# Folded K and V products made for two batches at once, evicted by ScalarE and GpSimd

## The chip, the cores and the metric

The kernel runs on one core of a Trainium2 chip. The metric is the device time of one execution in microseconds, lower is better. TensorE is called PE here, VectorE DVE, ScalarE ACT, GpSimd POOL and SyncE SP.

## What is computed

Cross attention and a quantised feed-forward block, each added to its input; x is 8 batches of 1024 tokens of 512 values, the context 8 batches of 64 tokens of 384 values, with 8 heads of 64.

```python
x = x + xattn(layernorm(x), ctx, Wq, Wk, Wv, Wo, bo)
x = x + ffn(layernorm(x), w_gate, w_up, w_down)

# xattn: q = x @ Wq, k = ctx @ Wk, v = ctx @ Wv, per head
#        softmax(q k^T / 8) v, heads joined, @ Wo + bo
# ffn:   bitlinear(silu(bitlinear(x, w_gate)) * bitlinear(x, w_up), w_down)
# bitlinear(x, w): x rounded to integers of -128..127 by its row's maximum,
#                  w rounded to -1, 0, 1 by its mean
```

Because k and v don't depend on x, the kernel folds them. For each batch it makes a 512 x 512 matrix from Wq and k (so that scores = x @ matrix) and one from v and Wo (so that the output = probabilities @ matrix). Each is held as a pair of 16-bit matrices, hi and lo, and so is each operand from x; three products (hi hi, hi lo, lo hi) replace one product in 32 bits.

## The kernel before

The 8192 tokens are 64 tiles of 128 rows, 8 tiles to a batch. After a setup (weights turned into -1, 0, 1, K and V made, first batches folded) a software pipeline runs steps s = -7 to 65. In step s the feed-forward tile is i = s and the attention tile is j = s + 6. Each engine runs one list of pieces in order; `queue` sorts the pieces by a due time, `at(s, f)` for fraction f of step s. A hand-written list, OPENING, comes ahead of everything else and reaches to about the end of step 4: a piece that it doesn't name runs after the whole of it. Engines meet only through semaphores.

A steady step has on PE, in this order: gate_up (tile i, part 0, 8 matmuls of 512 columns), scores (tile j, 12 matmuls), gate_up parts 1 and 2, attend (tile j - 1, 12), gate_up part 3, down (tile i - 1, 16 matmuls): 72 matmuls. DVE: `final` (L949, the last instruction on a tile, which adds the product of `down` to x), two `stats` (L943), `copy_h` (L979), `mult` and `h_part` of part 0 (L957, L961), `x_norm` (L985, normalised x for attention), `s_max` (L992, L996), `mult` part 1, `x_scale` (L1014 to L1022, for the quantised x), `h_part` 1, `e_sum` (L1002 to L1006), `mult` 2, `copy_x` (L1029), `h_part` 2, `add_x` (L1034), `mult` 3, `h_max`. ACT: `quant_h` (L738), `silu` 0 (L729), `x_hi` (L745), `silu` 1, `expo` (L749) between two table loads, `silu` 2, `quant_x` (L762), `p_hi` (L756), `silu` 3. POOL: `rstd` twice (L590, L592), `x_lo` (L598, needs `x_hi`), `add_bo` (L604, behind `x_lo` in the list), `p_norm` (L610), `p_lo` (L618). SP issues the loads, stores and transposes.

The folding of batches 1 to 7 is spread over the steps, one of eight rounds r of one batch at a time (r < 4 for K, r >= 4 for V). `load_bd` copies the batch's K or V by DMA into a block-diagonal tile with zeros (`kbd`, `vbd`), so that two heads of 64 fill 128 rows. `round_X` multiplies it on PE into the bank pX: 12 matmuls of 128 columns (K, L1161) or 3 of 512 (V, L1167). `hi` on ACT (L695) writes the high half, `lo` on DVE (L888) the low half. For b >= 2 round r belongs to step 8(b - 1) - 6 + r, so steps 2 to 49 have one each and steps 50 to 57 have none. On PE it comes after gate_up part 1, on DVE between `mult` 1 and `x_scale`. Steps are numbered here by their s; L949 in step s is `final` of tile s - 2.

Of the kernel before, what the change touches and what calls it, by code (L numbers as in the profile page):

```python
# [27 lines left out]
def xattn_ffn(nc, x, ctx_768, Wq, Wk, Wv, Wo, bo, w_gate, w_up, w_down, out):  # L28
# [11 lines left out]
    with ExitStack() as ctx:  # L40
# [19 lines left out]
        qbh = FF[:, 5120:6144].bitcast(BF16)  # L60
# [42 lines left out]
        mv1 = sb("mv1", [P, NT, 2], F32)  # L103
        mv2 = sb("mv2", [P, NT, 2], F32)
        ve1 = sb("ve1", [P, NT], F32)
        ve2 = sb("ve2", [P, NT], F32)
        rs1 = sb("rs1", [P, NT], F32)
        rs2 = sb("rs2", [P, NT], F32)
# [462 lines left out]
        def _(eng):  # L571
# [91 lines left out]
        def _(eng):  # L663
# [21 lines left out]
            def hi(b, r):  # L685
# [72 lines left out]
            def quant_x(t):  # L758
# [542 lines left out]
```

## Time and profile before

| | |
|---|---|
| time, median of 3 runs | 1141.64 us (1140.86 to 1144.83) |
| time of the profiled execution | 1140.11 us |
| its span (first to last instruction) | 1138.3 us |
| PE busy | 1089.3 us, 96% |
| DVE busy | 1060.4 us, 93% |
| ACT busy | 704.8 us, 62% |
| POOL busy | 449.9 us, 40% |

Busy PE time is modelled for pipelined matmuls and can't tell whether PE could go faster. The step is the unit to read in: the distance between two executions of L949.

### The profile page before, as it was taken

The page shows a single profiled execution, that of the slowest core. Times are in us where ns is not written, and L with a number is a line of the kernel's source. Part 1 is how long each engine was busy: PE and PEld are TensorE (multiplying, and loading weights), DVE is VectorE, ACT ScalarE, POOL GpSimd, SP SyncE. Part 2 cuts the span into 40 slices and gives each one's busy share as a digit, 9 for nine tenths or more (in the row PEclk, how much of TensorE's full clock was granted, in tenths as well). Part 3 has the DMA queues.
Part 4 walks back from the last instruction along what each step waited for, and adds up shares of the span by engine and source line. Part 5 has one row for each costly group of instructions (what it writes and reads, how often), then busy time and mean ns, then how long its engine had stood idle before and what let it go on. Part 6 is the DMA issues. An engine that isn't in the chain of part 4 may idle for free.

```text
span 1138.3 us, 17288 instructions
## 1 busy us (share of the span) xinstructions
PE 1089.3 (96%) x5212; PEld 506.2 (44%) x5274; DVE 1060.4 (93%) x2419; ACT 704.8 (62%) x891; POOL 449.9 (40%) x547
## 2 busy tenths in 40 slices
PE   5788998999999999999999999999999999999998
PEld 3444444444444444444444444444444444444443
DVE  6789997999999999999999999999999999999996
ACT  3786765666666666566656665666566656665543
POOL 2788341343344333434343434343334433443110
PEclk9889998999999999999999999999999999999999
DMA  9775953554555455555554564545545634554234
GB/s 353 219 190 107 158 106 80 107 116 98 102 115 114 91 109 113 111 98 107 116 110 100 102 121 100 109 102 121 100 96 111 120 93 103 107 111 88 66 84 97
DMA packets 358268, 132.48 MB, mean 116 GB/s; under 512 B 334752, under 2 KB 335264, under 8 KB 357664
## 3 DMA queue, kind: packets, MB, share of 16 engines
q1 hardware_dynamic: 358176, 131.39, 52.7%
q8 instruction: 42, 0.69, 0.2%
q14 instruction: 50, 0.41, 0.1%
HBM read 34.08 MB, written 16.78 MB: 45 GB/s over the span
## 4 chain that ended last, share of the span: by engine, by line
DVE 55%; PE 21%; issue 12%; ACT 3%; DMA 1%; DVEq 0%; POOL 0%; ACTq 0%; POOLq 0%
DVE FF L957 10%; PE ps L1235 9%; DVE hm L961 8%; DVE bns L943 5%; DVE FF L1014 4%; PE ps L1251 4%; DVE am L1015 3%; DVE xr L1034 3%; DVE den L1002 3%; DVE xr L949 2%; PE ps L1173 2%; PE ps L1174 2%; ACT FF L729 2%; PE ps L1176 2%; DVE xn L985 2%
## 5 line engine op out<-in xcount | busy, mean ns | idle before, releaser
L1235 PE MATMUL ps<-wgT,FF 128*128 128x512 bf16 x1024 | 263.2, 379 | 7.3 <-DMA FF<-FF 7.1
L1235 PE MATMUL ps<-wW,FF 128*128 128x512 bf16 x1024 | 262.8, 379 | 0.0
L738 ACT ACTIVATE FF<-FF,c 128x1024 int16<-128x1024 f32 x128 | 140.0, 1141 | 148.5 <-DVE c L971 148.5
L1251 PE MATMUL ps<-wW,FF 128*128 128x512 bf16 x962 | 220.4, 381 | 6.0 <-DMA FF<-FF 2.6
L729 ACT ACTIVATE FF<-ps,sg 128x512 f32<-128x512 f32 x256 | 172.1, 676 | 19.5 <-PE ps L1235 18.5
L961 DVE TENSOR_REDUCE hm<-FF 128x1 f32<-128x512 f32 x256 | 173.9, 680 | 4.4
L957 DVE TENSOR_TENSOR FF<-FF,ps 128x512 f32<-128x512 f32 x256 | 171.6, 672 | 1.2 <-PE ps L1235 0.9
L610 POOL TENSOR_TENSOR AT<-AT,rd 128x512 f32<-128x512 f32 x64 | 67.2, 1051 | 226.3 <-DVE rd L1006 226.3
L1251 PEld LDWEIGHTS ps<-wW,FF 128*128 128x128 bf16 x1024 | 100.4, 98 | 125.7 <-issue 7.7
L1235 PEld LDWEIGHTS ps<-wgT,FF 128*128 128x128 bf16 x1024 | 95.6, 98 | 132.0 <-DMA FF<-FF 26.7
L1235 PEld LDWEIGHTS ps<-wW,FF 128*128 128x128 bf16 x1024 | 100.0, 98 | 121.2 <-DVE FF L957 1.2
L590 POOL TENSOR_SCALAR ve<-mv 128x1 f32<-128x1 f32 x128 | 48.2, 376 | 265.6 <-DVE mv L944 265.6
L598 POOL TENSOR_TENSOR xhl<-xn,xhl 128x512 f16<-128x512 f32 x64 | 74.2, 1160 | 97.5 <-ACT xhl L745 97.5
L745 ACT ACTIVATE xhl<-xn 128x512 f16<-128x512 f32 x64 | 40.2, 629 | 110.5 <-DVE xn L985 109.7
L1173 PE MATMUL ps<-MV,pT 128*128 128x512 f16 x256 | 98.0, 383 | 3.5 <-issue 2.3
L1173 PE MATMUL ps<-MV,xT 128*128 128x512 f16 x256 | 98.0, 383 | 1.4 <-DMA xT<-xhl 0.9
L1174 PE MATMUL ps<-MV,pT 128*128 128x512 f16 x256 | 97.9, 383 | 0.0
L1174 PE MATMUL ps<-MV,xT 128*128 128x512 f16 x256 | 97.8, 382 | 0.0
L618 POOL TENSOR_TENSOR AT<-AT 128x512 f16<-128x512 f32 x64 | 74.2, 1159 | 50.7 <-POOL AT L610 43.7
L756 ACT ACTIVATE AT<-AT 128x512 f16<-128x512 f32 x64 | 40.3, 629 | 80.7 <-POOL AT L610 80.6
L592 POOL TENSOR_TENSOR rs<-ve,half 128x1 f32<-128x1 f32 x128 | 82.6, 645 | 10.7
L943 DVE BATCH_NORM_STATS2 bns<-xr 128x6 f32<-128x512 f32 x128 | 86.2, 674 | 0.0
(132 smaller groups left out, 1633.4 us busy)
## 6 DMA issues: line engine op xcount, KB each, us to landing
xr<-in_x SPq DMA_DIRECT2D x64, 256.0 KB, 2.8
out<-xr SPq DMA_DIRECT2D x64, 256.0 KB, 2.0
FF<-in_L_ffn_w_gate SPq DMA_DIRECT2D x4, 1024.0 KB, 12.6
wW<-in_L_ffn_w_up SPq DMA_DIRECT2D x4, 1024.0 KB, 13.2
FF<-in_L_ffn_w_down SPq DMA_DIRECT2D x4, 1024.0 KB, 6.0
FF<-FF SPq DMA_TRANSPOSE x192, 3.2
MV<-in_L_xattn_Wq SPq DMA_DIRECT2D x1, 1024.0 KB, 8.4
MV<-in_L_xattn_Wo SPq DMA_DIRECT2D x1, 1024.0 KB, 14.8
```

The lines of the kernel that those rows point to most:

```text
L592: eng.tensor_tensor(rs[:, t:t + 1], ve[:, t:t + 1], half[:, :], ALU.pow).then_inc(end, 1)
L598: eng.tensor_tensor(xhl[:, 1, :], xn[:, :], xhl[:, 0, :], ALU.subtract).then_inc(g_xl, 1)
L618: eng.tensor_tensor(phl[:, 1, :], E[:, j % 2, :], phl[:, 0, :], ALU.subtract).then_inc(g_pl, 1)
L729: eng.activation(h[:, i % 2, f * 512:(f + 1) * 512], G[n % 2][:, :], ACT.Silu, scale=sg[:, i:i + 1]).then_inc(a_si, 1)
L738: eng.activation(q16h[:, 1024 * z:1024 * z + 1024], h[:, t % 2, 1024 * z:1024 * z + 1024], ACT.Copy, scale=c2[:, t:t + 1]).then_inc(a_qh, 1)
L943: link(eng.bn_stats(bns[:, k, t % 2, :], xr[:, t % R, :]))
L957: eng.tensor_tensor(hh, hh, U[n % 2][:, :], ALU.mult).then_inc(v_h, 1)
L961: ins = eng.tensor_reduce(hm[:, f:f + 1], h[:, i % 2, f * 512:(f + 1) * 512], AX_X, ALU.max, apply_absolute_value=True)
L1173: eng.matmul(bank[:, :], T[:, k, :], hi[:, k, :], start=(k == 0), stop=False)
L1174: eng.matmul(bank[:, :], T[:, k, :], lo[:, k, :], start=False, stop=False)
L1235: mm = eng.matmul(bank[n % 2][:, :].rearrange("p (o f) -> p o f", o=4), qxT[:, i % 2, k, :], w[:, 4 * f:4 * f + 4, k, :], start=(k == 0), ...
L1251: mm = eng.matmul(y_bank(i)[:, :], hT[:, i % 2, c, :], wdT[:, c, :], start=(c == 0), stop=(c == 15))
```

## The change

Rounds of batches 2 to 7 are made for two batches (b, b + 1) at once, in 24 jobs: b = 2, 4, 6 and r = 0 to 7. Jobs of b = 4 lie in steps 18 to 25, of b = 6 in steps 34 to 41, of b = 2 in steps 4 to 10, with r = 6 and r = 7 both in step 10. Batches 0 and 1 are made as before.

- `pair_X` (PE) has no zeros and no copied operand. It multiplies half arrays: 64 rows of K or V of one head against 64 rows of the weights. K: 24 matmuls of 128 columns with 64 rows and 128 columns of the array, z = 0 and 1 in turn in the lower and the upper rows, into pY and pX. V: 12 matmuls of 512 columns with 64 x 64 of the array, four quarters in turn. It stands between gate_up part 0 and scores, and waits until `final` of the tile before has read pY and until the job before has been evicted.
- Eviction, for each of the two batches d: `j_wide` (ACT) copies the product to `wide_j` in 32 bits, with its scale (K: two instructions of 128x256, V: one of 128x512); `j_hi` (ACT) copies it to the 16-bit high half; `j_lo` (POOL) subtracts to the low half. `j_wide` of d = 1 waits for `j_lo` of d = 0, since `wide_j` is one tile. On ACT the order is silu 0, j_wide 0, j_hi 0, x_hi, j_wide 1, silu 1, j_hi 1, expo; on POOL rstd, rstd, j_lo 0, x_lo, add_bo, j_lo 1, p_norm.
- For b >= 2, `load_bd` (24 DMAs), `round_X`, `hi` and `lo` are gone; `down` also waits until jobs of its step and earlier are evicted.
- The folded matrices have three slots in place of two (`chunk`); room comes from `kbd`, `vbd` and other setup tiles inside S2, from `qbh` laid over `q16h` (so `quant_h` waits for the transposes of the tile before, which `copy_h` waited for), and from per-tile scalars kept for 8 tiles in place of 64 (indices % W, left out below).
- Steps 2, 3, 11 to 17, 26 to 33 and 42 to 49 have no folding left.

```diff
-        qbh = FF[:, 5120:6144].bitcast(BF16)
+        qbh = FF[:, 4096:5120].bitcast(BF16)
...
+        wide_j = FF[:, 9728:10240]
...
+        def chunk(b, k, c):
+            o = 1024 * k + 256 * c
+            if b % 3 < 2:
+                m = MV[:, 4096 * (b % 3) + o:4096 * (b % 3) + o + 256]
+            elif k < 3:
+                m = S2[:, o:o + 256]
+            else:
+                m = FF[:, 5120 + 256 * c:5376 + 256 * c]
+            return m.bitcast(F16)
...
-        kbd = sb("kbd", [P, 4, 2, P], F16)
-        vbd = sb("vbd", [P, 4, 2, P], F16)
+        S2 = sb("S2", [P, 3072], F32)
+        kbd, vbd = [S2[:, 512 * n:512 * n + 512].bitcast(F16).rearrange("p (q y l) -> p q y l", q=4, y=2)
+                    for n in range(2)]
...
+        pYX = ctx.enter_context(nc.psum_tensor("ps6", [P, 1024], F32))
         G, U = PS[0:2], PS[2:4]
-        pS, pA, pY, pX = PS[4], PS[5], PS[6], PS[7]
+        pS, pA, pY, pX = PS[4], PS[5], pYX[:, 0:512], pYX[:, 512:1024]
...
+            return at(r // 4, r % 4 * .25 - .3)
+        def job_step(b, r):
+            return PAIR_S.get((b, r), TPB * (b - 1) - L + r)
+        def job(b, r):
+            return 8 * (b // 2 - 1) + r
+        PAIR_S = {(2, r): (4, 5, 6, 7, 8, 9, 10, 10)[r] for r in range(8)}
+        JOB_F = (0.266, (0.324, 0.399), (0.388, 0.623))
+        JOBS = [(b, r) for b in range(2, NB, 2) for r in range(8)]
+        def job_at(b, r, f):
+            return at(job_step(b, r), f + (.24 if r and job_step(b, r - 1) == job_step(b, r) else 0))
...
-            for b in range(1, NB):
-                put(jit_at(b, 0) - (8 if b > 1 else 30), load_bd, b, 0)
-                put(jit_at(b, 3) + (6 if b > 1 else -29), load_bd, b, 1)
+            put(jit_at(1, 0) - 30, load_bd, 1, 0)
+            put(jit_at(1, 3) - 29, load_bd, 1, 1)
...
+            def j_lo(b, r, d):
+                n = 2 * job(b, r) + d
+                k = 2 * (r // 4)
+                eng.wait_ge(a_jh, n + 1)
+                eng.tensor_tensor(chunk(b + d, k + 1, r % 4), wide_j, chunk(b + d, k, r % 4),
+                                  ALU.subtract).then_inc(g_jl, 1)
...
+            for b, r in JOBS:
+                put(job_at(b, r, JOB_F[2][0]), j_lo, b, r, 0)
+                put(job_at(b, r, JOB_F[2][1]), j_lo, b, r, 1)
...
+            def j_wide(b, r, d):
+                n = 2 * job(b, r) + d
+                eng.wait_ge(p_J, job(b, r) + 1)
+                if n >= 1:
+                    eng.wait_ge(g_jl, n)
+                scale = fwd[:, r // 4, b + d:b + d + 1]
+                if r >= 4:
+                    eng.activation(wide_j, (pY, pX)[d], ACT.Copy, scale=scale).then_inc(a_jw, 2)
+                else:
+                    for z in range(2):
+                        src = (pY, pX)[z].rearrange("p (q b l) -> p q b l", q=4, b=2)[:, :, d, :]
+                        dst = wide_j.rearrange("p (q z l) -> p q z l", q=4, z=2)[:, :, (z + d) % 2, :]
+                        eng.activation(dst, src, ACT.Copy, scale=scale).then_inc(a_jw, 1)
+            def j_hi(b, r, d):
+                n = 2 * job(b, r) + d
+                eng.wait_ge(a_jw, 2 * n + 2)
+                if r % 4 == 0 and d == 0:
                     eng.wait_ge((p_S, p_A)[r // 4], TPB * (b - 1))
-                eng.activation(part(b, 2 * (r // 4))[:, r % 4, :], bank_of(n)[:, :], ACT.Copy,
-                               scale=fwd[:, r // 4, b:b + 1]).then_inc(a_hi, 1)
+                eng.activation(chunk(b + d, 2 * (r // 4), r % 4), wide_j, ACT.Copy).then_inc(a_jh, 1)
...
-                    eng.wait_ge(v_qh, 2 * t + z - 1)
+                    eng.wait_ge(t_h[(t - 1) % 2][z], 16 * ((t - 1) // 2 + 1))
...
-                for r in range(8):
-                    put(jit_at(b, r) + 7.14, hi, b, r)
+            for r in range(8):
+                put(jit_at(1, r) + 7.14, hi, 1, r)
+            for b, r in JOBS:
+                for d, w in enumerate(JOB_F[1]):
+                    put(job_at(b, r, w), j_wide, b, r, d)
+                    put(job_at(b, r, w + .005), j_hi, b, r, d)
...
-            for b in range(1, NB):
-                for r in range(8):
-                    put(jit_at(b, r) + 7.99, lo, b, r)
+            for r in range(8):
+                put(jit_at(1, r) + 7.99, lo, 1, r)
...
+            def pair_X(b, r):
+                n = job(b, r)
+                if n == 0:
+                    eng.wait_ge(v_lo, 16)
+                else:
+                    eng.wait_ge(a_jw, 4 * n)
+                eng.wait_ge(v_y, job_step(b, r) - 1)
+                for q in range(4) if r < 4 else (r - 4,):
+                    for x, y in ((0, 0), (0, 1), (1, 0)):
+                        for z in range(2):
+                            h0 = slice(64 * z, 64 * z + 64)
+                            if r < 4:
+                                mm = eng.matmul((pY, pX)[z][:, q * P:(q + 1) * P], wqT[h0, x, q, r * P:(r + 1) * P],
+                                                split[0][h0, q, y, b * LC:(b + 2) * LC], start=(x + y == 0), stop=(x == 1))
+                            else:
+                                for d in range(2):
+                                    o = 64 * ((z + d) % 2)
+                                    mm = eng.matmul((pY, pX)[d][o:o + 64, :],
+                                                    split[1][h0, q, x, (b + d) * LC:(b + d + 1) * LC], wo[h0, y, q, :],
+                                                    start=(x + y == 0), stop=(x == 1))
+                mm.then_inc(p_J, 1)
...
+            def folded_done(b, m):
+                if b < 2:
+                    eng.wait_ge(v_lo, 8 * b + 4 * m + 4)
+                else:
+                    eng.wait_ge(g_jl, 2 * job(b - b % 2, 4 * m + 3) + 2)
...
+                    done = sum(job_step(b, r) <= i + 1 for b, r in JOBS)
+                    if done:
+                        eng.wait_ge(a_jw, 4 * done)
...
-            for b in range(1, NB):
-                for r in range(8):
-                    put(jit_at(b, r) + 6.46, round_X, b, r)
+            for r in range(8):
+                put(jit_at(1, r) + 6.46, round_X, 1, r)
+            for b, r in JOBS:
+                put(job_at(b, r, JOB_F[0]), pair_X, b, r)
```

## Rows read from the trace of the kernel before

**Rows 1.** The page, part 1: busy us (share of the span) xinstructions.

```profile
PE 1089.3 (96%) x5212; PEld 506.2 (44%) x5274; DVE 1060.4 (93%) x2419; ACT 704.8 (62%) x891; POOL 449.9 (40%) x547
```

**Rows 2.** Windows of three steps (first has a round; columns stand in its first line).

```profile
core 0: us, PE busy (x) PEld busy (x) DVE busy (x) ACT busy (x) POOL busy (x), PEclk, DMA share, GB/s
574.25:590.55 16.30, 16.25 (x85) 7.58 (x84) 15.78 (x37) 10.35 (x14) 6.46 (x8) 1.00 0.49 106
966.34:982.64 16.30, 15.66 (x73) 6.97 (x72) 15.78 (x36) 9.76 (x12) 6.46 (x8) 1.00 0.51 106
982.64:998.95 16.31, 15.00 (x70) 6.67 (x69) 15.79 (x36) 9.76 (x13) 6.46 (x8) 1.00 0.54 102
```

**Rows 3.** Timeline, start and duration in us: a step without a round, three engines.

```profile
982.64 0.74 DVE L949 SCALAR_TENSOR_TENSOR xr<-ps,sd,xr 128x512 f32<-128x512 f32 x1
...
984.74 0.67 ACT L729 ACTIVATE FF<-ps,sg 128x512 f32<-128x512 f32 x1
...
985.78 0.56 POOL L592 TENSOR_TENSOR rs<-ve,half 128x1 f32<-128x1 f32 x1
...
986.89 0.54 DVE L985 TENSOR_SCALAR xn<-xr,mv,rs 128x512 f32<-128x512 f32 x1
...
987.46 0.63 ACT L745 ACTIVATE xhl<-xn 128x512 f16<-128x512 f32 x1 [2.06 <-DVE xn L985]
...
988.00 0.67 ACT L729 ACTIVATE FF<-ps,sg 128x512 f32<-128x512 f32 x1
...
988.17 1.16 POOL L598 TENSOR_TENSOR xhl<-xn,xhl 128x512 f16<-128x512 f32 x1 [1.84 <-ACT xhl L745]
...
989.29 1.27 POOL L604 TENSOR_TENSOR xr<-xr,bo_sb 128x512 f32<-128x512 f32 x1
989.31 1.53 DVE L1014 TENSOR_SCALAR FF<-xr,mv 128x512 f32<-128x512 f32 x1
...
992.02 0.69 ACT L729 ACTIVATE FF<-ps,sg 128x512 f32<-128x512 f32 x1
...
993.95 3.40 PE L1251 MATMUL ps<-wW,FF 128*128 128x512 bf16 x15
994.04 0.65 DVE L957 TENSOR_TENSOR FF<-FF,ps 128x512 f32<-128x512 f32 x1
```

**Rows 4.** Timeline: a step with a round, `lo` and the `x_scale` behind it.

```profile
557.95 0.74 DVE L949 SCALAR_TENSOR_TENSOR xr<-ps,sd,xr 128x512 f32<-128x512 f32 x1
...
564.61 0.74 DVE L888 SCALAR_TENSOR_TENSOR MV<-ps,fwd,MV 128x512 f16<-128x512 f32 x1
...
565.27 0.87 DVE L1014 TENSOR_SCALAR FF<-xr,mv 128x512 f32<-128x512 f32 x1
```

**Rows 5.** Timeline of the setup: an `x_norm` that meets a POOL instruction.

```profile
103.11 1.15 POOL L618 TENSOR_TENSOR AT<-AT 128x512 f16<-128x512 f32 x1
103.14 1.40 DVE L985 TENSOR_SCALAR xn<-xr,mv,rs 128x512 f32<-128x512 f32 x1
```

**Rows 6.** Groups of instructions by line: busy us, mean ns of one.

```profile
L888 DVE SCALAR_TENSOR_TENSOR MV<-ps,fwd,MV 128x512 f16<-128x512 f32 x64 | 47.6, 746 | 11.2 <-ACT MV L695 10.9
L695 ACT ACTIVATE MV<-ps,fwd 128x512 f16<-128x512 f32 x64 | 43.6, 684 | 15.7 <-PE ps L1161 12.2 <-PE ps L1167 3.1
...
L738 ACT ACTIVATE FF<-FF,c 128x1024 int16<-128x1024 f32 x128 | 140.0, 1141 | 148.5 <-DVE c L971 148.5
```

**Rows 7.** Timeline: PE in a K round and in a V round.

```profile
579.30 0.83 PE L1161 MATMUL ps<-kbd,wqT 128*128 128x128 f16 x12
...
269.02 0.81 PE L1167 MATMUL ps<-wo,vbd 128*128 128x512 f16 x3
```

**Rows 8.** Timeline of step 4: three rounds one behind another ahead of `down`.

```profile
185.89 0.83 PE L1161 MATMUL ps<-kbd,wqT 128*128 128x128 f16 x12
...
186.76 0.69 ACT L695 ACTIVATE MV<-ps,fwd 128x512 f16<-128x512 f32 x1 [2.17 <-PE ps L1161]
...
192.52 1.06 PE L1251 MATMUL ps<-wW,FF 128*128 128x512 bf16 x2 [0.22 <-issue]
...
192.92 0.68 ACT L729 ACTIVATE FF<-ps,sg 128x512 f32<-128x512 f32 x1
```

**Rows 9.** Windows around it, columns as in rows 2.

```profile
188.00:190.80 2.80, 0.83 (x12) 0.69 (x12) 0.98 (x2) 0.69 (x1) 0.00 (x0) 0.80 0.21 38
190.80:197.70 6.90, 6.62 (x27) 3.37 (x29) 3.55 (x9) 2.27 (x3) 0.00 (x0) 0.58 0.01 2
```

More of the change, by code:

```diff
@@ L16 @@
 R = 11
+W = 8
 ALU = mybir.AluOpType
@@ L102, in xattn_ffn @@
         bns = sb("bns", [P, 2, 2, 6], F32)
[L103 to L108, printed above, removed]
+        mv1 = sb("mv1", [P, W, 2], F32)
+        mv2 = sb("mv2", [P, W, 2], F32)
+        ve1 = sb("ve1", [P, W], F32)
+        ve2 = sb("ve2", [P, W], F32)
+        rs1 = sb("rs1", [P, W], F32)
+        rs2 = sb("rs2", [P, W], F32)
         mx = sb("mx", [P, 2, 8], F32)
@@ L138, in xattn_ffn @@
         half = sb("half", [P, 1], F32)
-        PS = [ctx.enter_context(nc.psum_tensor(f"ps{n}", [P, 512], F32)) for n in range(8)]
+        PS = [ctx.enter_context(nc.psum_tensor(f"ps{n}", [P, 512], F32)) for n in range(6)]
+        pYX = ctx.enter_context(nc.psum_tensor("ps6", [P, 1024], F32))
         G, U = PS[0:2], PS[2:4]
-        pS, pA, pY, pX = PS[4], PS[5], PS[6], PS[7]
+        pS, pA, pY, pX = PS[4], PS[5], pYX[:, 0:512], pYX[:, 512:1024]
         l_ctx = sem("l_ctx")
@@ L196, in xattn_ffn @@
         p_fl = sem("p_fl")
+        p_J = sem("p_J")
+        a_jw = sem("a_jw")
+        a_jh = sem("a_jh")
+        g_jl = sem("g_jl")
         a_ft = sem("a_ft")
@@ L589, in rstd @@
                 eng.wait_ge(done, t + 1)
-                eng.tensor_scalar(ve[:, t:t + 1], mv[:, t, 1:2], EPS, None, ALU.add).then_inc(mid, 1)
+                eng.tensor_scalar(ve[:, t % W:t % W + 1], mv[:, t % W, 1:2], EPS, None, ALU.add).then_inc(mid, 1)
                 eng.wait_ge(mid, t + 1)
-                eng.tensor_tensor(rs[:, t:t + 1], ve[:, t:t + 1], half[:, :], ALU.pow).then_inc(end, 1)
+                eng.tensor_tensor(rs[:, t % W:t % W + 1], ve[:, t % W:t % W + 1], half[:, :], ALU.pow).then_inc(end, 1)
             def x_lo(t):
@@ L692, in hi @@
                     setup_done(eng, SETUP - 1)
-                if b >= 2 and r % 4 == 0:
+                eng.activation(chunk(b, 2 * (r // 4), r % 4), bank_of(n)[:, :], ACT.Copy,
+                               scale=fwd[:, r // 4, b:b + 1]).then_inc(a_hi, 1)
+            def j_wide(b, r, d):
[15 more added lines that the diff above has]
+                if r % 4 == 0 and d == 0:
                     eng.wait_ge((p_S, p_A)[r // 4], TPB * (b - 1))
-                eng.activation(part(b, 2 * (r // 4))[:, r % 4, :], bank_of(n)[:, :], ACT.Copy,
-                               scale=fwd[:, r // 4, b:b + 1]).then_inc(a_hi, 1)
+                eng.activation(chunk(b + d, 2 * (r // 4), r % 4), wide_j, ACT.Copy).then_inc(a_jh, 1)
             def abs_sum(m, c):
@@ L761, in quant_x @@
                     eng.wait_ge(v_qx, t)
-                eng.activation(q16x, xc2, ACT.Copy, scale=c1[:, t:t + 1]).then_inc(a_qx, 1)
+                eng.activation(q16x, xc2, ACT.Copy, scale=c1[:, t % W:t % W + 1]).then_inc(a_qx, 1)
             for r in ON_ACT:
@@ L943, in stats @@
                 link(eng.bn_stats(bns[:, k, t % 2, :], xr[:, t % R, :]))
-                eng.bn_aggr(mv[:, t, :], bns[:, k, t % 2, :]).then_inc(done, 1)
+                eng.bn_aggr(mv[:, t % W, :], bns[:, k, t % 2, :]).then_inc(done, 1)
             def final(t):
@@ L948, in final @@
                 eng.wait_ge(v_sd, t + 1)
-                eng.scalar_tensor_tensor(out=xr[:, t % R, :], in0=y_bank(t)[:, :], scalar=sd[:, t:t + 1],
+                eng.scalar_tensor_tensor(out=xr[:, t % R, :], in0=y_bank(t)[:, :], scalar=sd[:, t % W:t % W + 1],
                                          in1=xr[:, t % R, :], op0=ALU.mult, op1=ALU.add).then_inc(v_y, 1)
@@ L1182, in scores @@
                 if j % TPB == 0:
-                    eng.wait_ge(v_lo, 8 * b + 4)
+                    folded_done(b, 0)
                 if j >= 1:
                     eng.wait_ge(v_sub, j)
-                three(pS, xT[:, j % 2, :, :], part(b, 0), part(b, 1)).then_inc(p_S, 1)
+                three(pS, xT[:, j % 2, :, :], [chunk(b, 0, k) for k in range(4)],
+                      [chunk(b, 1, k) for k in range(4)]).then_inc(p_S, 1)
             def attend(j):
@@ L1196, in attend @@
                     eng.wait_ge(v_x1, j)
-                three(pA, pT[:, j % 2, :, :], part(b, 2), part(b, 3)).then_inc(p_A, 1)
+                three(pA, pT[:, j % 2, :, :], [chunk(b, 2, k) for k in range(4)],
+                      [chunk(b, 3, k) for k in range(4)]).then_inc(p_A, 1)
             def total(m):
```

81 lines of the change are left out of this document (36 added, 45 removed), and 9 rows, old and new, of the table OPENING.

## The prediction, made before the changed kernel was run

> **What bounds the kernel now.** The page's busy shares come first: PE 96%, DVE 93% [rows 1]. They suggest that work taken from PE or DVE shortens the kernel, and this change takes a `lo` from DVE 48 times, 746 ns each [rows 6], and halves PE's streaming of the folding if its half arrays run side by side. So I looked next for steps that already lack this work: steps 50 to 57 have no round. The windows show it plainly: the step with a round took 16.30 us, two steps without one 16.30 and 16.31 [rows 2]. PE had work for 72 matmuls at 0.216 us (of 15 recorded, 3.40 us less the 0.38 of one, over 14 [rows 3]), 15.55 us, at the full granted clock of 1.00 [rows 2]. So PE isn't what sets 16.30 there. DVE was busy 15.78 us with 37 instructions and 15.79 with 36 [rows 2]: one fewer, and no less busy.
>
> The timelines say why. Without a round `x_scale`'s first instruction, L1014, took 1.53 us; with one it took 0.87, behind a `lo` of 0.74 [rows 3, 4]. In both steps it ends 8.20 us after the step's L949, and 0.28 after POOL's `add_bo` (989.29 + 1.27 = 990.56, against 990.84) [rows 3]. DVE waits there for POOL to finish. The loop that sets the step is thus: L949, DVE's list up to `x_norm` (dispatched 4.25 us later), `x_hi` on ACT, `x_lo` and `add_bo` on POOL, L1014, and then DVE's list back to back for 8.1 us to the next L949. `lo` lies inside the wait and costs nothing.
>
> By this the trace agrees with the Trainium skill, SBUF (State Buffer), "Who interferes with whom": a DVE instruction in a 2-port mode and a GpSimd one exclude each other for a whole instruction. The numbers above don't need it.
>
> **What is removed.** `lo`: 0 in a steady step, since the cover stays. If POOL's chain were shorter, up to 0.67 a step (0.746 less the overlap). `round_X` on PE (0.83 and 0.81 us, of which 0.22 and 0.16 is the last one's latency [rows 7]): 0 as well, as steps 50 to 57 have none and take 16.30. `hi` on ACT, the 24 DMAs on SP: 0; ACT isn't in the loop at that point and no chain step waits for them. Steps 11 to 17, 26 to 33 and 42 to 49 so stay at 16.30. The slots, `qbh` over `q16h` and the scalars % W cost 0: the transpose that `quant_h` now waits for was issued a step earlier.
>
> **What a job adds to its step.** I lay it over the step without a round [rows 3] in the order of the new lists. On PE `pair_X` must wait for L949 (ends 983.38) and is over by about 984.7 to 985.2, so the first product is there when silu 0 ends (985.41). Then, on ACT:
> - V: j_wide 0, as `hi` 0.68 [rows 6], 985.32 to 986.00; j_hi 0, as `x_hi` 0.63, to 986.65; POOL's j_lo 0 0.08 behind it as `x_lo` is behind `x_hi` [rows 3], so 986.73 to 987.89 (1.16, as `x_lo`). `x_norm` is dispatched at 986.89 and finds POOL at work. The setup shows that very pair: `x_norm` took 1.40 us and ended 0.28 after POOL [rows 5]. It ends at 988.17 in place of 987.43, and `x_hi`, `x_lo`, `add_bo` and L1014 all move by it: +0.75 us.
> - K: j_wide 0 is two instructions of 256 columns. Between 512 and 1024 columns ACT pays 0.46 us [rows 6], so one of 256 is about 0.45, two about 0.85 with their overlap. j_hi 0 ends at 986.82, POOL could begin at 986.90, just behind `x_norm`. Then `x_norm` is free, j_lo 0 runs 987.43 to 988.59 and `x_lo` starts 0.40 late: +0.40 us. If POOL wins this tie it is +0.92 (988.06 + 0.28 against 987.43). I take 0.40, because a strided read of PSUM can only be later.
>
> Behind it on ACT, j_wide 1 (0.68) waits for j_lo 0 and stands ahead of silu 1, so silu 1 comes 1.4 us late. `mult` 1 then ends near 990.8: still before L1014 would be released by `add_bo` (991.3), the wait that `lo` filled before hides it. silu 2 (992.02) is 1.9 to 2.0 us late, needed by `mult` 2 at 994.04 plus the shift [rows 3]; that just holds. j_lo 1 starts when `add_bo` ends and is done long before `p_norm`.
>
> **PE's share.** K streams 12 pairs at (0.83 - 0.22)/11 = 0.055 us each, 0.66 us if lower and upper halves overlap, 1.32 if not. V: 0.65 if all four quarters overlap, 1.30 for two, 2.59 for none (3, 6 or 12 times 0.216). No row shows a change of array shape. I bound both changes together between 0 and 0.5 us (twice the 0.16 of latency and 0.1 of weight load), and take 0.3. The room in a job step is 16.30 + 0.40 or 0.75 - 15.55, so 1.15 to 1.50. With overlap it needs about 0.95 and costs nothing further.
>
> **The two odd places.** Step 10 has two V jobs. The second one's j_wide 0 and j_hi 0 stand before silu 2 (1.2 us, `mult` 2 late by 1.1), j_wide 1 and j_hi 1 before silu 3 (about 0.4 more): with the 0.75 it costs 2.3 us. In step 4 the reverse: OPENING ends there, and three `round_X` stand one behind another on PE, each waiting for the `hi` and `lo` before it; `down` starts 6.63 us after the first one (192.52 - 185.89) [rows 8]. After, one job is there and `down` waits for its j_wide 1: 0.87 to the first eviction, then 0.85 + 0.65 + 1.2 + 0.85, near 190.4 and so 2.1 earlier; silu 3, at 192.92 before, comes 1.9 earlier. I take -1.9. PE's granted clock was 0.80 and then 0.58 over these stretches [rows 9], after its pauses; if the single pause of some 3.5 us keeps the clock up, `down` saves 2 us more, so -3.9 is the other end, and 0 the upper one.
>
> **Sum.** 11 single K jobs x 0.40 = 4.4 (steps 5 to 7, 18 to 21, 34 to 37); 10 single V jobs x 0.75 = 7.5 (8, 9, 22 to 25, 38 to 41); step 10, 2.3; step 4, -1.9. Together +12.3, on the profiled execution's 1140.1: 1152.4. The median of the runs lies 1.5 above that execution, so I predict 1154. With all singles at 0.40 and step 4 at -3.9 it is 1148; with all K at 0.92 and step 4 at 0, 1162.
>
> **Rivals.**
> 1. *Handover hidden.* POOL is idle from 986.34 to 988.17 [rows 3], 1.83 us, which would hold j_lo 0's 1.16. If it doesn't block `x_norm`, jobs cost 0, step 10 about 0.5, step 4 gives -1.9: 1138.7 + 1.5 = 1140. Against it: `x_norm` in the setup and L1014 [rows 3, 5]. Chance 0.20.
> 2. *Quarters overlap by halves.* PE in a V step needs 15.55 + 1.30 + 0.5 = 17.35, 0.3 over the 17.05 of the sum, times 12: 1158. Chance 0.12. The Trainium skill, TensorEngine Tiling (Array Packing), "Gotcha 1: PSUM Pressure", speaks for this one: different row tiles can't use the same PSUM bank at once, and the V job sends lower and upper rows of one d to one bank. No row here shows a row tile.
> 3. *The half arrays don't overlap*, so that the change doesn't do what it says. K steps need 15.55 + 1.32 + 0.5 = 17.37, +1.07; V steps 15.55 + 2.59 + 0.5 = 18.64, +2.34; step 10 +5.4: 11.8 + 23.4 + 5.4 - 1.9 = +38.7, 1180. PE becomes the bound. Chance 0.08.
> 4. *Faster.* DVE's 0.67 shows in the 23 free steps from 11 to 49, because POOL's chain isn't the loop but only coincides with it: -15.4 - 1.9 and +0.5, near 1125. Against it: 16.30 in steps that lack the work. Chance 0.08.
>
> **How the numbers follow.** The forecast above, 1154 with 1148 to 1162 as its own range, has a chance of 0.52. The range, 1139 to 1168, takes in rivals 1 and 2 and leaves out 3 and 4. 0.5%, about what a measurement of this kernel can tell from no change, is 5.7 us. Slower: 0.52 + 0.12 + 0.08 = 0.72. Same: 0.20. Faster: 0.08.
>
> **What would show it.** In the profile after: L949 to L949 16.3 in steps 11 to 17, 26 to 33 and 42 to 49, and 16.7 or 17.05 in job steps; L985 at 1.2 to 1.4 us in V jobs, 0.54 in K jobs; L1014 always ending 0.28 after `add_bo`; the V matmuls of a job done in 0.7 us beside their latency (2.6 without overlap); `down` of step 4 starting 4.5 us after the job began. Free steps below 16.2 would refute the loop that I read; job steps at 16.3 the block of `x_norm`; gaps on DVE before `mult` 2 would mean that ACT's list, not POOL, became the bound.

## The result, and the profile after

The changed kernel took 1160.26 us (1159.16 to 1162.69, 4 runs) beside 1143.24 us (1140.86 to 1147.05, 4 runs) for the kernel before: a ratio of 1.0149 [1.0114, 1.0184], slower. Forecast were 1154 and a range of 1139 to 1168. The profiled execution took 1160.23 us, with a span of 1158.4 us, 20.1 more than before. In the changed kernel `final` is L1009, `mult` L1017, `x_norm` L1043, `x_scale` L1072, `x_lo` L625, `add_bo` L631, `j_lo` L662, `j_wide` L740 (V) and L746 (K), `j_hi` L753, `x_hi` L802, `pair_X` L1242 (K) and L1247 (V), `down` L1343.

The page of the changed kernel, parts 1 and 4 (busy us, share and instructions; then the shares of the chain that ended last), answers to [rows 1]. PE lost 5.0 us of busy time, DVE gained 3.8 with 48 instructions fewer, ACT and POOL gained 29.8 and 57.5:

```profile
PE 1084.3 (94%) x5284; PEld 493.9 (43%) x5346; DVE 1064.2 (92%) x2371; ACT 734.6 (63%) x963; POOL 507.4 (44%) x595
DVE 60%; issue 15%; PE 11%; ACT 8%; DMA 2%; POOL 2%; DVEq 0%; SPq 0%; ACTq 0%; POOLq 0%
```

The windows of the changed kernel, one step each, answer to [rows 2]: first a step without a job, then a K job's and a V job's.

```profile
core 0: us, PE busy (x) PEld busy (x) DVE busy (x) ACT busy (x) POOL busy (x), PEclk, DMA share, GB/s
386.49:402.79 16.30, 15.68 (x73) 6.93 (x72) 15.78 (x36) 9.76 (x12) 6.46 (x8) 1.00 0.47 105
419.08:436.26 17.18, 16.61 (x97) 7.57 (x96) 15.98 (x36) 12.36 (x18) 8.90 (x10) 1.00 0.59 101
487.83:504.86 17.03, 16.61 (x85) 7.19 (x84) 15.84 (x36) 12.06 (x16) 8.90 (x10) 1.00 0.55 102
```

The step without a job is the free step of before to the last digit, 16.30 us. The job steps are longer by 0.88 and 0.73, and DVE's busy time grows only by 0.20 and 0.06. That doesn't price the waits: DVE is counted busy while it waits for POOL inside an instruction, so the busy time holds both a longer `x_norm` and a shorter L1072 (timelines below). By distances between two executions of L1009:

| steps | before | after | forecast |
|---|---|---|---|
| without a job (11 to 17, 26 to 33, 42 to 56) | 16.30, a few up to 16.57 | 16.30; 11, 43, 51: 16.48; 27: 16.76 | 16.30 |
| K jobs 5 to 7 | 16.69, 16.30, 16.55 | 17.09, 17.19, 17.18 | 16.70 |
| K jobs 18 to 21 (34 to 37 within 0.01) | 16.30 (19: 17.02) | 17.18, 17.37, 17.01, 17.19 | 16.70 |
| V jobs 8, 9, 22 to 25, 38 to 41 | 16.30 (41: 16.53) | 17.03 to 17.05 | 17.05 |
| step 10, two V jobs | 16.30 | 18.71 | 18.6 |
| step 4 | 16.98 | 16.08 | 15.1 |
| start to the first `final` | 148.05 | 151.65 | no change |

The timeline of a V job's step in the changed kernel (start, duration; in brackets the engine's idle time ahead and what ended it) answers to [rows 3]:

```profile
487.83 0.74 DVE L1009 SCALAR_TENSOR_TENSOR xr<-ps,sd,xr 128x512 f32<-128x512 f32 x1
488.72 0.84 PE L1247 MATMUL ps<-wo,vT 64*64 64x512 f16 x12
489.49 0.39 PE L1254 MATMUL ps<-MV,xT 128*128 128x512 f16 x1
490.49 0.68 ACT L740 ACTIVATE FF<-ps,fwd 128x512 f32<-128x512 f32 x1
491.20 0.63 ACT L753 ACTIVATE MV<-FF 128x512 f16<-128x512 f32 x1
491.91 1.15 POOL L662 TENSOR_TENSOR MV<-FF,MV 128x512 f16<-128x512 f32 x1 [0.40 <-ACT MV L753]
492.06 1.28 DVE L1043 TENSOR_SCALAR xn<-xr,mv,rs 128x512 f32<-128x512 f32 x1
493.38 0.63 ACT L802 ACTIVATE xhl<-xn 128x512 f16<-128x512 f32 x1 [1.55 <-DVE xn L1043]
494.08 1.16 POOL L625 TENSOR_TENSOR xhl<-xn,xhl 128x512 f16<-128x512 f32 x1 [1.02 <-ACT xhl L802]
495.19 0.69 DVE L1017 TENSOR_TENSOR FF<-FF,ps 128x512 f32<-128x512 f32 x1 [0.53 <-ACT FF L786]
495.20 1.28 POOL L631 TENSOR_TENSOR xr<-xr,bo_sb 128x512 f32<-128x512 f32 x1
495.80 0.96 DVE L1072 TENSOR_SCALAR FF<-xr,mv 128x512 f32<-128x512 f32 x1
496.42 1.35 POOL L662 TENSOR_TENSOR FF<-FF,S 128x512 f16<-128x512 f32 x1
```

`j_lo` 0 begins 4.08 us after L1009, `x_norm` is dispatched 0.15 us after that, finds POOL at work, takes 1.28 us in place of 0.54 and ends at 493.34, 5.51 after L1009; in [rows 3] it ends 4.79 after it. Everything behind it moves by that 0.72: `x_hi`, `x_lo`, `add_bo`, and L1072, which ends 0.28 after `add_bo` as before (495.20 + 1.28 = 496.48, against 496.76). In the step without a job of [rows 3] POOL's slot was empty there. The same place in a K job's step:

```profile
419.08 0.74 DVE L1009 SCALAR_TENSOR_TENSOR xr<-ps,sd,xr 128x512 f32<-128x512 f32 x1
419.97 0.85 PE L1242 MATMUL ps<-kT,wqT 64*128 64x128 f16 x24
421.74 0.82 ACT L746 ACTIVATE FF<-ps,fwd 128x256 f32<-128x256 f32 x2
422.60 0.63 ACT L753 ACTIVATE MV<-FF 128x512 f16<-128x512 f32 x1
423.31 1.16 POOL L662 TENSOR_TENSOR MV<-FF,MV 128x512 f16<-128x512 f32 x1 [0.55 <-ACT MV L753]
423.31 1.43 DVE L1043 TENSOR_SCALAR xn<-xr,mv,rs 128x512 f32<-128x512 f32 x1
```

This is the tie of which the prediction spoke. Both begin in the same hundredth, and POOL goes first: `x_norm` ends 5.66 after L1009, 0.87 late. Eight of the eleven K steps look like this, POOL at 4.22 or 4.23 us after L1009 and `x_norm` at 4.22 to 4.24. In steps 20 and 36 POOL begins 0.2 us ahead (4.05 and 4.04), and `x_norm` ends 0.17 to 0.18 earlier. In step 5 `x_norm` is dispatched early, 3.44 us after its `final`, and is free; there the block falls on L1072, by `j_lo` 1, which has begun at 208.16 (start and duration):

```profile
204.06 0.54 DVE L1043 TENSOR_SCALAR xn<-xr,mv,rs 128x512 f32<-128x512 f32 x1
208.22 1.39 DVE L1072 TENSOR_SCALAR FF<-xr,mv 128x512 f32<-128x512 f32 x1
```

### The profile page after: what moved, and what is told of

Its sections match the earlier page's. It is cut to its first block, busy times and chain, and to the rows that moved or that the text cites. A ratio compares the mean times of both kernels' runs of the same rounds, so it can differ in the third digit from the quotient of the medians.

```text
span 1158.4 us, 17323 instructions
## 1 busy us (share of the span) xinstructions
PE 1084.3 (94%) x5284; PEld 493.9 (43%) x5346; DVE 1064.2 (92%) x2371; ACT 734.6 (63%) x963; POOL 507.4 (44%) x595
## 4 chain that ended last, share of the span: by engine, by line
DVE 60%; issue 15%; PE 11%; ACT 8%; DMA 2%; POOL 2%; DVEq 0%; SPq 0%; ACTq 0%; POOLq 0%
DVE hm L1021 9%; DVE FF L1017 8%; DVE bns L1003 6%; DVE FF L1072 6%; DVE xn L1043 4%; PE ps L1324 4%; DVE FF L1037 4%; DVE xr L1092 3%; DVE am L1073 3%; DVE xr L1009 3%; ACT FF L786 3%; DVE den L1060 3%; ACT xhl L802 2%; PE ps L1343 1%; DVE mv L1004 1%
## 5 line engine op out<-in xcount | busy, mean ns | idle before, releaser
L795 ACT ACTIVATE FF<-FF,c 128x1024 int16<-128x1024 f32 x128 | 140.0, 1140 | 147.8 <-DVE c L1031 147.8
L1343 PE MATMUL ps<-wW,FF 128*128 128x512 bf16 x962 | 221.0, 382 | 11.7 <-issue 6.0
L1017 DVE TENSOR_TENSOR FF<-FF,ps 128x512 f32<-128x512 f32 x256 | 171.9, 674 | 20.7 <-ACT FF L786 18.9
L1021 DVE TENSOR_REDUCE hm<-FF 128x1 f32<-128x512 f32 x256 | 173.9, 680 | 4.4
L1343 PEld LDWEIGHTS ps<-wW,FF 128*128 128x128 bf16 x1024 | 100.5, 98 | 131.9 <-issue 14.0
L625 POOL TENSOR_TENSOR xhl<-xn,xhl 128x512 f16<-128x512 f32 x64 | 74.1, 1158 | 78.2 <-ACT xhl L802 78.2
L802 ACT ACTIVATE xhl<-xn 128x512 f16<-128x512 f32 x64 | 40.2, 629 | 97.5 <-DVE xn L1043 96.7
L631 POOL TENSOR_TENSOR xr<-xr,bo_sb 128x512 f32<-128x512 f32 x64 | 81.7, 1276 | 6.6 <-DVE xn L1043 6.5
L1254 PE MATMUL ps<-MV,pT 128*128 128x512 f16 x192 | 73.3, 382 | 3.7 <-issue 2.4
L1254 PE MATMUL ps<-MV,xT 128*128 128x512 f16 x192 | 72.9, 380 | 1.4 <-DMA xT<-xhl 0.9
```

Of the source, the lines that this page charges most:

```text
L625: eng.tensor_tensor(xhl[:, 1, :], xn[:, :], xhl[:, 0, :], ALU.subtract).then_inc(g_xl, 1)
L631: eng.tensor_tensor(xr[:, t % R, :], xr[:, t % R, :], bo_sb[:, :], ALU.add).then_inc(g_xb, 1)
L1017: eng.tensor_tensor(hh, hh, U[n % 2][:, :], ALU.mult).then_inc(v_h, 1)
L1021: ins = eng.tensor_reduce(hm[:, f:f + 1], h[:, i % 2, f * 512:(f + 1) * 512], AX_X, ALU.max, apply_absolute_value=True)
L1254: eng.matmul(bank[:, :], T[:, k, :], hi[k], start=(k == 0), stop=False)
L1343: mm = eng.matmul(y_bank(i)[:, :], hT[:, i % 2, c, :], wdT[:, c, :], start=(c == 0), stop=(c == 15))
```

## Experiments

The question left by the traces is whether POOL's work for `j_lo` 0 is the cause or only stands beside it. Rivals: ACT's longer list (silu 1 comes late, L1017 at 495.19 waited 0.53 us for it), PE's work for the job, or a DVE loop that takes 16.30 whatever POOL does.

### j_lo behind x_lo (e1_late_lo)

The changed kernel with `j_lo` 0 behind `x_lo` and `add_bo` on POOL, and with `j_wide` 1 behind silu 1 on ACT, in all jobs but those of step 10.

```diff
-        JOB_F = (0.266, (0.324, 0.399), (0.388, 0.623))
+        JOB_F = (0.266, (0.324, 0.65), (0.5, 0.85))
+        JOB_10 = (0.266, (0.324, 0.399), (0.388, 0.623))
+        def job_f(b, r):
+            return JOB_10 if job_step(b, r) == 10 else JOB_F
```

> The changed kernel with j_lo 0 moved behind x_lo on GpSimd, j_lo 1 behind p_lo, and j_wide 1 and j_hi 1 moved behind quant_x on ScalarE (all but step 10, whose two jobs stay as they are). Theory A, GpSimd's j_lo 0 ahead of x_lo costs the job steps their time, by blocking x_norm and delaying x_lo: the 21 single job steps fall from 17.04 to 17.38 us to 16.3, x_norm is back at 0.54, and the kernel comes to about 1143 us. Theory B, TensorE sets the job steps (15.55 us and about 0.85 for the job): they fall to 16.4 only, 1146. Theory C, ScalarE's four more instructions cost the time wherever they stand: job steps stay at 16.9 or more, 1155 or more.

Measured: 1149.63 us (1147.63 to 1149.71), 1.0043 [1.0027, 1.006] of before, where the change had 1.0149. The steps of the K and V jobs from 18 on take 16.30 (19 and 35: 16.48). Three steps don't, the last single job's of each group (9, 25 and 41), with 17.41. With step 10, which this edit leaves at 18.70, they are most of what the time lies over Theory A's 1143. PE's work is the same as in the changed kernel, so PE isn't what makes its job steps 17.0 to 17.4. Both POOL's and ACT's lists were changed here, and e5, below, separates them. Windows of e1, a job's step and step 25, and the timeline of the latter:

```profile
467.80:484.10 16.30, 16.25 (x96) 7.55 (x95) 15.43 (x37) 12.59 (x19) 8.86 (x10) 1.00 0.48 105
533.00:550.40 17.40, 17.28 (x88) 7.49 (x88) 15.78 (x37) 12.39 (x17) 8.67 (x10) 1.00 0.57 99
...
537.22 0.54 DVE L1047 TENSOR_SCALAR xn<-xr,mv,rs 128x512 f32<-128x512 f32 x1
539.61 1.27 POOL L635 TENSOR_TENSOR xr<-xr,bo_sb 128x512 f32<-128x512 f32 x1
540.27 0.69 DVE L1021 TENSOR_TENSOR FF<-FF,ps 128x512 f32<-128x512 f32 x1 [0.73 <-PE ps L1328]
540.83 1.16 POOL L666 TENSOR_TENSOR MV<-FF,MV 128x512 f16<-128x512 f32 x1
540.88 1.40 DVE L1076 TENSOR_SCALAR FF<-xr,mv 128x512 f32<-128x512 f32 x1
```

`x_norm` (L1047 here) is free, 0.54 us, 4.78 after its `final`. PE is full in a job's step, 16.25 of 16.30 us. `mult` 1 (L1021) waited for PE, and so L1076 was dispatched 0.05 us after `j_lo` 0 had taken POOL, and paid 1.40. Why this strikes the last of a group: PE needs 16.42 in a job's step (e3, below) where DVE's loop gives it 16.30, so it falls back 0.12 a step. The trace shows that: `mult` 1 begins 6.33, 6.45, 6.57, 6.68 and 6.81 us after `final` in steps 20 to 24. In step 25 it begins at 7.29, of which 0.36 is more than this drift; e3's free steps 17 and 33 have the same 0.36, and its cause is open. Together they carry L1076 past the start of `j_lo` 0.

### Without j_lo 0 (e5_no_lo0)

The order of the changed kernel stays, ACT's list too, but the first of the two `j_lo` isn't made.

```diff
             def j_lo(b, r, d):
+                if d == 0:
+                    return
...
-                if n >= 1:
-                    eng.wait_ge(g_jl, n)
+                if d == 0 and n >= 1:
+                    eng.wait_ge(g_jl, n // 2)
+                elif d == 1:
+                    eng.wait_ge(a_jh, n)
```

> The changed kernel without j_lo 0: GpSimd's subtraction for the even batch of each job is left out, and batches 2, 4 and 6 use their high halves in place of the low ones, so their attention is computed with wrong low parts. ScalarE's list is untouched (all four instructions, ahead of silu 1), only j_wide 1 no longer waits for GpSimd. Theory A: job steps 16.3 to 16.4 us, x_norm at 0.54, kernel 1142 to 1146 us. Theory C (ScalarE's list ahead of silu 1): job steps stay above 16.8, vector engine idle ahead of mult 1 as before.

Measured: 1146.23 us (1144.27 to 1147.89, 10 runs), 1.0023 [1.0011, 1.0035]. From 18 on, job steps take 16.35 to 16.42 (19 and 35: 16.53), step 10 takes 18.03, and 9, 25 and 41 take 17.47. ACT's list stays late here: silu 1 begins 6.02 and silu 2 10.57 us after `final` (step 22), 0.66 and 1.19 later than in [rows 3]. In the changed kernel they begin 1.29 and 1.81 later, of which 0.73 is the step's own shift. Without that shift the silus are as late in e5 as in the changed kernel, and the steps are short. That refutes ACT's list as the cause and leaves POOL's one instruction. In step 25 of e5 what catches L1076 is `j_lo` 1, again by hundredths:

```profile
533.57 0.54 DVE L1047 TENSOR_SCALAR xn<-xr,mv,rs 128x512 f32<-128x512 f32 x1
537.25 1.16 POOL L664 TENSOR_TENSOR FF<-FF,S 128x512 f16<-128x512 f32 x1
537.27 1.42 DVE L1076 TENSOR_SCALAR FF<-xr,mv 128x512 f32<-128x512 f32 x1
```

### The loop of the kernel before (e2_before_late_bo)

The kernel before, with `add_bo` moved from behind `x_lo` to the end of the step.

```diff
-                    put(norm_at(s, .41, "lo"), add_bo, j + 1)
+                    put(norm_at(s, .41, "lo") if s < 0 else at(s, .9), add_bo, j + 1)
```

> The kernel before with one edit: add_bo of the tiles from 12 on is put behind p_lo in GpSimd's list (due .9 in place of .41). Theory A says that GpSimd's add_bo releases L1014 and so sets the 16.30 us of every steady step: steps 50 to 57, which have no round, fall to about 15.6 to 15.8, what TensorE's 72 matmuls need; steps 5 to 49, which have one, fall little (16.2 to 16.3), because TensorE needs 15.55 + 0.75 there. About 1135 us in all. Theory D, the wait of L1014 only coincides with the loop and something else sets 16.30: no step changes, 1142 us.

Measured: 1133.81 us (1132.3 to 1135.93), 0.9911 [0.9892, 0.993]. Windows of e2, a step with a round and one without, and L1014 of the latter:

```profile
559.22:575.42 16.20, 16.15 (x85) 7.69 (x85) 15.48 (x37) 10.45 (x14) 6.47 (x8) 1.00 0.48 105
994.29:1009.83 15.54, 15.49 (x72) 7.06 (x72) 14.92 (x36) 9.69 (x13) 6.32 (x8) 1.00 0.49 109
...
1001.08 0.48 DVE L1014 TENSOR_SCALAR FF<-xr,mv 128x512 f32<-128x512 f32 x1
```

L1014 takes 0.48 us in place of 1.53 [rows 3], and the free step takes 15.54 us, what 72 matmuls need by the prediction's 15.55. So DVE has no loop of 16.30 of its own; `add_bo` made it. With it gone PE sets the step, and a round costs 0.66 us (16.20 - 15.54).

### Both (e3_both_late)

e1's edit and e2's in the changed kernel.

> The changed kernel with both edits: j_lo, j_wide 1 and j_hi 1 late (as in the run of the late j_lo) and add_bo late. Theory A: free steps 15.6 to 15.8 us, job steps 16.4 (TensorE in both), about 31 x 0.6 us less than the late j_lo alone: 1125 us, less than the kernel before and less than the kernel before with late add_bo, so that the folding for two batches at once pays once GpSimd is out of the loop. Theory D: 1143 us. If TensorE's saving were lost in another wait, it would be no faster than the kernel before with late add_bo.

Measured: 1119.55 us (1119.25 to 1124.41), 0.9795 [0.977, 0.9819], faster than both kernels, and 14.3 us under e2. Not all of that is the change's: in the profiles the steps from 5 on add up to 916.62 us in e3 and 926.48 in e2, 9.9 less, while 4.6 lie ahead of the first `final` (149.16 against 153.80), which scatters from run to run (last experiment). Windows of e3: a free step, a K job's, a V job's; then the V matmuls, `x_norm` and L1076 of one step:

```profile
360.03:375.57 15.54, 15.49 (x72) 7.06 (x72) 14.88 (x35) 9.76 (x13) 6.45 (x8) 1.00 0.60 111
439.50:455.92 16.42, 16.37 (x96) 7.65 (x96) 15.02 (x35) 12.51 (x19) 8.68 (x11) 1.00 0.48 107
505.18:521.60 16.42, 16.37 (x84) 7.23 (x84) 14.96 (x36) 12.35 (x17) 8.69 (x11) 1.00 0.49 105
...
490.38 0.84 PE L1251 MATMUL ps<-wo,vT 64*64 64x512 f16 x12
493.01 0.54 DVE L1047 TENSOR_SCALAR xn<-xr,mv,rs 128x512 f32<-128x512 f32 x1
496.36 0.48 DVE L1076 TENSOR_SCALAR FF<-xr,mv 128x512 f32<-128x512 f32 x1
```

Every step now goes by PE, and a job's price on PE can be read for the first time: 16.42 - 15.54 = 0.88 us for a round of two batches, where e2 pays 0.66 for one. Of the 0.88, 0.66 (K) or 0.65 (V) is streaming as the prediction had it, so the two changes of the array's shape, and what else stands around them, take 0.22 to 0.23.

### add_bo late alone (e7_after_late_bo)

The changed kernel with e2's edit only.

> The changed kernel with add_bo late and j_lo left where the change puts it. In the run with both late the vector engine's loop had about 1 us of room in a step (15.54 us with L1014 unblocked, 16.42 in a job step, which TensorE sets). Theory A: x_norm is still blocked by j_lo 0 in job steps (1.2 to 1.4 us, later by 0.75), and j_lo 1 now follows x_lo directly and can block L1014 as add_bo did, so job steps come to 16.4 at best and 17.0 at worst; free steps 15.54. Kernel 1121 to 1134 us. If the order of j_lo doesn't matter once add_bo is late, it equals the run with both late, 1119.6.

Measured: 1145.12 us (1142.55 to 1147.76, 10 runs), 1.0018 [1.0006, 1.003]. My expectation was 11 us or more too low. Free steps take 15.54 and less (a few up to 15.68), but the job steps got longer, K 17.60 to 17.96 from 18 on, V 17.48. Timeline of e7, a V job's step:

```profile
507.19 1.15 POOL L662 TENSOR_TENSOR MV<-FF,MV 128x512 f16<-128x512 f32 x1 [0.40 <-ACT MV L753]
507.35 1.28 DVE L1043 TENSOR_SCALAR xn<-xr,mv,rs 128x512 f32<-128x512 f32 x1
511.04 1.15 POOL L662 TENSOR_TENSOR FF<-FF,S 128x512 f16<-128x512 f32 x1 [0.52 <-ACT S L753]
511.08 1.40 DVE L1072 TENSOR_SCALAR FF<-xr,mv 128x512 f32<-128x512 f32 x1
```

Both POOL instructions of the job now catch a DVE instruction; L1072 was dispatched 0.04 us after the second had begun. In the changed kernel `add_bo` stood in that place and caught L1072 as well, but ended earlier: `j_lo` 1 has to wait for ACT's `j_hi` 1 and ends 9.07 us after `final`, `add_bo` ended 8.65 after it. The 0.42 is nearly all that a V job's step is longer by than in the changed kernel (17.48 against 17.04); my bound of 17.0 had left it out. Neither edit alone gets what both get.

### Order of the half arrays (e4_tiles_in_turn, e6_columns_only)

To test the overlap on PE I put the half arrays in turn, in e3, where PE is the bound: in e4 all of the lower rows first, then the upper ones, and in V each quarter's three matmuls in a row; in e6 likewise, but in V the two column halves alternate.

```diff
-                for q in range(4) if r < 4 else (r - 4,):
-                    for x, y in ((0, 0), (0, 1), (1, 0)):
-                        for z in range(2):
-                            h0 = slice(64 * z, 64 * z + 64)
-                            if r < 4:
+                for z in range(2):
+                    h0 = slice(64 * z, 64 * z + 64)
+                    if r < 4:
+                        for q in range(4):
+                            for x, y in ((0, 0), (0, 1), (1, 0)):
```

> The kernel with both late, with the products of a job in another order: all 12 (K) or 6 (V) matmuls of the lower rows first and then those of the upper rows, and for V each quarter's three one behind another. TensorE sets the steps here, so the job's cost is read from the step: 16.42 - 15.54 = 0.88 for K and V now. If half arrays overlap only when they alternate: K 24 x 0.055 = 1.32 plus 0.2, so steps of 17.05; V 12 x 0.216 = 2.59 plus 0.2, steps of 18.3. If the hardware looks ahead far enough or the overlap doesn't hang on the order, they stay at 16.42.

> As the tiles in turn, but for V the two column halves of the same rows alternate, so that only quarters in the same rows can overlap. K as in the tiles in turn. If column halves overlap when they alternate, V is 6 x 0.216 = 1.30 plus 0.2, steps of 17.05; if only row halves overlap, 18.3.

Measured: e4 1129.28 us, 0.9879 [0.9858, 0.99]; e6 1127.08 us, 0.986 [0.9839, 0.9881]; both slower than e3's 1119.55. The steps from 5 on make 5.3 us of either difference (921.93 and 921.91 against 916.62), the rest lies ahead of them. The PE groups, K and V, of e4 and then of e6:

```profile
431.00 1.31 PE L1246 MATMUL ps<-kT,wqT 64*128 64x128 f16 x24
481.65 0.86 PE L1253 MATMUL ps<-wo,vT 64*64 64x512 f16 x12
...
429.04 1.31 PE L1246 MATMUL ps<-kT,wqT 64*128 64x128 f16 x24
479.69 0.85 PE L1253 MATMUL ps<-wo,vT 64*64 64x512 f16 x12
```

K lost most of its overlap, 1.31 in place of 0.85 us, and its steps take 16.89 in place of 16.42. That is 0.46 of the 0.66 that a full loss would cost (the 17.05 of the expectation), so some overlap was left. V, for which longer steps were expected, lost nothing: 0.86 and 0.85 us, and steps of 16.43 to 16.44 in both. So two blocks of twelve matmuls, one in each half, overlap only in part, while the V matmuls overlap fully whether each quarter has its three in a row (e4) or the two lower quarters alternate for six and then the two upper ones (e6). K and V differ in shape, width and block length at once, so which of these decides is open.

### The two kernels again (b0_again, a0_again)

For the 3.6 us by which the first `final` came later:

> The kernel before once more, unchanged, for its profile. The first final came 3.6 us later in the profile of the changed kernel than in that of before (151.65 and 148.05), and at 149.2 to 153.9 in the four variants run so far, whose setup is the same. If this is scatter of the setup from run to run, it lies somewhere between 148 and 154 here too, and the steady steps are 16.30; if before always has 148.05, the change costs its 3.6 us in the setup.

> The changed kernel unedited, for the 3.6 us by which its first execution of the final addition came later than in the kernel before (151.65 us against 148.05). If that is scatter of the start, it comes anywhere from 148 to 154 us here, while the steps stay: K jobs of steps 18 to 21 within 0.3 us of 17.18, 17.37, 17.01 and 17.19, V jobs at 17.0 to 17.1, step 10 at 18.7. If it is the changed setup, it comes at 151.3 to 152.0 again, and the span is 1158 to 1159.

Measured: 1142.03 and 1161.44 us. The first `final` began at 150.21 in the kernel before and at 153.69 in the changed one. With before's setup (before, b0_again, e2) it lies at 148.05, 150.21 and 153.80, with the changed one at 149.16 (e3) to 153.87 (e1) in eight profiles. The spread within each is wider than the difference, so the 3.6 can be scatter; a share of 1 to 2 us for the changed setup can't be excluded. The changed kernel's steps from 5 on came back within 0.03 us (17.20, 17.38, 17.01, 17.19 in 18 to 21), and step 4 didn't: 15.01 in place of 16.08 (before: 17.11 and 16.98).

## Why the prediction was right, and where its terms were off

- **What bounds the kernel.** Right. Free steps stayed at 16.30, and e2, which takes the block of L1014 by `add_bo` away, shows that it holds them there. Rival 4, that DVE's 0.67 a step would show, is refuted.
- **`lo`, `round_X`, `hi` removed: 0.** Right, for the reason given. Behind a shorter POOL chain it is `round_X` on PE that would have shown, and not `lo` on DVE as I wrote: with `add_bo` late PE sets every step, a round costs 0.66 there (e2) and a free step is rid of it (16.20 against 15.54).
- **V job, +0.75.** Measured +0.74, by the same instruction pair as in [rows 5]. e1 and e5 take the block away in two ways, and the 0.74 is gone in seven of the ten steps; the three last ones of a group pay 1.1 to 1.2 for another block, at L1076.
- **K job, +0.40.** The mis-sized term: 0.70 to 1.08, mean 0.88 over 16.30. The step that failed is the tie: that `x_norm` is free held in one K job of eleven, step 5, and there it didn't help, since `j_lo` 1 caught L1072 instead (+0.79 over 16.30, +0.40 over the 16.69 of before, which matches the forecast by luck). My lead for `x_norm` was 0.01 us (986.89 against 986.90); `j_wide` 0 took 0.82 against 0.85 estimated, which was enough to lose it. That the strided read "can only be later" had nothing behind it. My upper end, 0.92, was close to the value in the eight ties. Steps 19 and 35 hold 0.18 that isn't the job's: 11, 43 and 51 have it without one. Eleven jobs make 9.7 us in place of 4.4.
- **Step 10, +2.3.** Measured +2.41.
- **Step 4, -1.9.** -0.90 in the profiled execution and -2.1 between a0_again and b0_again, so one pair can't tell. The windows of the changed kernel around `down`, and `down` itself:

```profile
189.50:194.60 5.10, 0.92 (x26) 0.81 (x27) 0.83 (x2) 2.76 (x6) 1.15 (x1) 0.84 0.39 78
194.60:200.40 5.80, 5.80 (x15) 2.15 (x15) 2.25 (x7) 2.95 (x4) 1.91 (x3) 0.55 0.00 0
194.60 5.98 PE L1343 MATMUL ps<-wW,FF 128*128 128x512 bf16 x15 [4.18 <-issue]
```

  and `down` of the same step in e2, whose step 4 is that of the kernel before:

```profile
197.49 3.40 PE L1251 MATMUL ps<-wW,FF 128*128 128x512 bf16 x15
```

  `down` began 5.03 us after the job (forecast 4.5; 4.64 in a0_again) and ran at a granted clock of 0.55, 5.98 us for 15 matmuls. In a0_again its 16 took 5.30. The hope of -3.9, that one pause keeps the clock up, fell: after a pause of 4.18 us the granted clock was 0.55 over the 5.8 us of `down`, most of it at the lower of the two levels (1.2 of 2.4 GHz), as after the three pauses of before [rows 9]; in a0_again it was 0.65. But in e2 the same three pauses left it at 1.00: `down` took 3.40 us and step 4 15.14, where before and b0_again had 16.98 and 17.11. So step 4 moves by 2 us with the clock alone, and the forecast of -1.9 is neither confirmed nor refuted.
- **The sum.** From the first to the last `final` the kernel takes 1003.36 us in place of 986.51, +16.85, against +12.3 forecast. The terms as measured are 9.7 (K), 7.4 (V), 2.4 (step 10) and -0.9 (step 4), together 18.6; steps 5, 7, 19 and 41 of before, which were 1.6 us over 16.30 already, leave 17.0, and the free steps add up to the same in both within 0.1. K alone is worth 5.3 more than I had put down. The medians differ by 17.0, in agreement. I had put the base of the sum at 1141.64; the kernel before had 1143.24 beside the changed one, which makes 1.6 of the 6.3 us by which 1154 was too low. The scatter from run to run also shows what is weak in building on one execution: the one of before lay 3 us under the median of 1143.24 that ran beside the changed kernel.
- **Rivals 2 and 3.** Refuted. Twelve matmuls of 512 columns in 0.84 us are 3 x 0.216 and 0.19 of latency: all four quarters run at once. In e3, where PE sets the step, a V job adds 0.88 in all, less than the 1.30 that two at a time would stream. By the Trainium skill, TensorEngine Tiling (Array Packing), "Gotcha 1: PSUM Pressure", lower and upper rows of one d couldn't have met in one bank; the trace doesn't agree, and the measurement decides.
- **Rival 1, handover hidden.** Refuted: `x_norm` is blocked in every job step but 5. Its price of 1140 was too low as well: with `j_lo` 0 gone altogether (e5) the kernel takes 1146.23, 1.0023 of before, and most of what lies over a plain 0 is in steps 9, 25 and 41 (1.17 each) and step 10 (1.7 in place of 0.5).

## What to carry to other kernels

Before work is taken from the busiest engine, look for steps that already lack it; if they take as long, the work is cover for a wait, and the wait is what to remove first (`add_bo` late is worth 0.9% by itself, and with it gone and `j_lo` out of the way the change is worth some 0.9% more, the 9.9 us from step 5 on in e3 against e2). Here a piece moved to GpSimd cost what the VectorE instruction that met it had to wait, which hung on where it started to a tenth of a microsecond: put it beside a VectorE instruction that isn't blocked (in the V job's rows L1017 took its 0.69 beside `add_bo`) or inside a wait that is there anyway. Where a forecast turns on a tie between two engines, price both outcomes and don't take the cheaper one.

## What the runs showed of the hardware

- A DVE instruction that meets one on POOL ends 0.28 to 0.29 us after it (492.06 + 1.28 against 491.91 + 1.15; 540.88 + 1.40 against 540.83 + 1.16), so in these rows it loses one POOL instruction and no more. Two in a row don't hold it off: in the V job's step L1072 ran between `add_bo` and `j_lo` 1, and it was `j_lo` 1 that took 1.35 in place of 1.15.
- Of two that start in the same hundredth (423.31), POOL went first, as in all eight K steps whose two starts lie within 0.02 us of each other.
- Half arrays of 64 rows and 128 columns that alternate give 24 matmuls of 128 columns in 0.85 us, 0.055 us for each pair and so 0.027 for each; quarters give 12 of 512 columns in 0.84 us, and 0.85 and 0.86 in the two other orders tried. A change of the array's shape and back costs no more than 0.22 to 0.23 us together (0.88 less 0.66 or 0.65).
- TensorE's granted clock after the same three pauses was 0.58 in one run [rows 9] and 1.00 in another (e2), 5.38 and 3.40 us for 15 matmuls of `down`.
